# Six per-row scalars allocated in front of the transposed keys: every fp32r matmul operand starts on a multiple of 256 bytes

## The reference

```python
x_norm = (x - mu) / sqrt(var + EPS) * gamma + beta
q, k, v = x_norm @ qkv[:, :512], x_norm @ qkv[:, 512:1024], x_norm @ qkv[:, 1024:]
attn = softmax(where(causal, q @ k.T / sqrt(512), -inf))
x1 = layernorm(x + (attn @ v @ o_proj + x))
route = softmax(x1 @ wr.T); gates, idx = top_2(route), gates / sum
h2 = silu(silu(x1 @ w1.T) @ w3.T);  h = h2 @ w2.T
out = zeros; out[idx[:, k]] += gates[:, k] * h        # only rows 0 to 7 of 8192
return layernorm(x1 + out)
```

## Time and profile before

| | us |
|---|---|
| median of 3 executions | 1724.53 |
| lowest, highest | 1723.97, 1726.92 |
| span of the profiled execution | 1729.0 |
| TensorE (PE) busy in it | 1697.6 |
| VectorE, ScalarE, GpSimd busy | 788.8, 670.0, 282.0 |

### The profile page before, as it was taken

How to read it: one execution, slowest core, us unless ns; L and a number is a source line. 1 busy time by engine, 2 the same in 40 slices (tenths; PEclk the granted TensorE clock), 3 DMA queues, 4 the chain that set the end, 5 groups by cost and what they waited for, 6 DMA issues and landing times.

```text
span 1729.0 us, 23965 instructions
## 1 busy us (share of the span) xinstructions
PE 1697.6 (98%) x8179; PEld 1400.9 (81%) x8179; DVE 788.8 (46%) x2104; ACT 670.0 (39%) x1301; POOL 282.0 (16%) x491
## 2 busy tenths in 40 slices
PE   7999999999999999999999999999999999999998
PEld 5888888878888887888888888888878888888886
DVE  5454433455353454445344554534444443444443
ACT  4443333343342344334224433423344444444442
POOL 1220201121120111112011211201122121212111
PEclk9999999999999999999999999999999999999999
DMA  4111201121110112121111222112230101010100
GB/s 152 56 49 50 68 31 37 62 82 60 56 68 31 37 60 70 61 68 55 43 37 49 73 68 68 49 40 72 87 103 25 49 24 49 24 49 24 49 0 7
DMA packets 50116, 92.58 MB, mean 54 GB/s; under 512 B 5456, under 2 KB 5456, under 8 KB 50016
## 3 DMA queue, kind: packets, MB, share of 16 engines
q1 hardware_dynamic: 38064, 70.31, 11.8%
q10 hardware_dynamic: 11952, 20.99, 3.9%
HBM read 57.71 MB, written 33.57 MB: 53 GB/s over the span
## 4 chain that ended last, share of the span: by engine, by line
PE 82%; issue 12%; POOL 2%; ACT 2%; DVE 1%; DMA 1%; POOLq 0%; SPq 0%; ACTq 0%; DVEq 0%
PE psum L330 24%; PE psum L332 24%; PE psum L331 24%; PE psum L1186 3%; PE psum L1278 1%; PE psum L1124 1%; PE psum L1288 1%; PE psum L1296 1%; PE psum L1295 1%; PE psum L1287 1%; POOL expo L510 1%; POOL rstd L435 1%; ACT xin L561 1%; DMA raw<-in_wk_t 1%; ACT affine L545 0%
## 5 line engine op out<-in xcount | busy, mean ns | idle before, releaser
L330 PE MATMUL psum<-xt_hi,g_hi 128*128 128x512 f32 (+3 forms) x640 | 242.4, 379 | 0.4 <-DVE g_lo L834 0.4
L332 PE MATMUL psum<-xt_lo,g_hi 128*128 128x512 f32 (+3 forms) x640 | 232.0, 362 | 0.0
L331 PE MATMUL psum<-xt_hi,g_lo 128*128 128x512 f32 (+3 forms) x640 | 230.8, 361 | 0.0
L609 ACT ACTIVATE pt_hi<-psum 128x512 fp32r<-128x512 f32 (+3 forms) x160 | 84.8, 531 | 373.3 <-PE psum L1186 366.0
L330 PE MATMUL psum<-v_hi,pt_hi 128*128 128x512 f32 x544 | 223.0, 410 | 1.6 <-DVE pt_lo L844 1.1
L332 PE MATMUL psum<-v_lo,pt_hi 128*128 128x512 f32 x544 | 213.3, 392 | 0.0
L331 PE MATMUL psum<-v_hi,pt_lo 128*128 128x512 f32 x544 | 212.7, 391 | 0.0
L432 POOL TENSOR_TENSOR var_eps<-meanvar,eps 128x2 f32<-128x2 f32 (+1 forms) x97 | 19.3, 199 | 1070.2 <-DVE meanvar L812 1065.7
L849 DVE TENSOR_REDUCE rowmax<-psum 128x1 f32<-128x512 f32 (+3 forms) x160 | 97.7, 611 | 201.7 <-PE psum L332 200.9
L731 ACT ACTIVATE act_f<-psum 128x512 f32<-128x512 f32 x128 | 76.6, 598 | 241.4 <-PE psum L332 241.4
L510 POOL TENSOR_TENSOR expo<-euler,shifted 128x32 f32<-128x32 f32 x16 | 87.3, 5455 | 325.1 <-DVE shifted L1036 325.1
(11 more groups left out here) (146 smaller groups left out, 3379.6 us busy)
## 6 DMA issues: line engine op xcount, KB each, us to landing
xin<-in_x ACTq DMA_DIRECT2D x64, 256.0 KB, 2.8
tok<-in_x SPq DMA_DIRECT2D x64, 256.0 KB, 2.6
x_scratch<-tok SPq DMA_DIRECT2D x64, 256.0 KB, 2.1
out_dram<-tok SPq DMA_DIRECT2D x64, 256.0 KB, 2.0
x_in<-x_scratch SPq DMA_DIRECT2D x14, 1024.0 KB, 5.5
xin<-in_w_t ACTq DMA_DIRECT2D x8, 256.0 KB, 2.8
x_in<-x_scratch ACTq DMA_DIRECT2D x2, 1024.0 KB, 7.8
w_sb<-in_w_t SPq DMA_DIRECT2D x1, 1024.0 KB, 5.7
```

The costliest lines, as they stand in the source:

```text
L330: pe.matmul(o, ws, ms, start=first, stop=False, skip_group_check=True)
L331: pe.matmul(o, w_lo, ms, start=False, stop=False, skip_group_check=True)
L332: return pe.matmul(o, ws, m_lo_, start=False, stop=last, skip_group_check=True)
L609: act.activation(pt_hi[:, n % 2, 0:w], psum[:, turn_bank(turn_use(t, c)), 0:w], ACT.Copy).then_inc(pt_hi_ready, 1)
```

## The change

The six small tensors move from behind `tok` to in front of `xt_hi`. In stage 2 an unused tensor `row_scalars` of 48 floats (192 bytes, as much as the six take) holds their place, and the filler is 64 floats shorter.

```diff
+    ROW_SCALARS = 6 * 8
...
-        xt_hi = sb("xt_hi", [P, DC, S], F32R, stage01)
-        xt_lo = sb("xt_lo", [P, DC, S], F32R, stage01)
-        affine = sb("affine", [P, 512], F32, stage01)
-        tok = sb("tok", [P, SLOTS, D], F32, stage01)
         rowmax4 = sb("rowmax4", [P, 4], F32, stage01)
         rowmax = sb("rowmax", [P, 1], F32, stage01)
         bias = sb("bias", [P, 2], F32, stage01)
         sums4 = sb("sums4", [P, 2, 4], F32, stage01)
         rowsum = sb("rowsum", [P, 1], F32, stage01)
         rinv = sb("rinv", [P, 2], F32, stage01)
+        xt_hi = sb("xt_hi", [P, DC, S], F32R, stage01)
+        xt_lo = sb("xt_lo", [P, DC, S], F32R, stage01)
+        affine = sb("affine", [P, 512], F32, stage01)
+        tok = sb("tok", [P, SLOTS, D], F32, stage01)
...
+        sb("row_scalars", [P, ROW_SCALARS], F32, stage2)
         x1_in = sb("x1_in", [P, 2, GROUP, D], F32, stage2)
...
-        sb("not_yet_free", [P, 2 * DC * S - taken + (1 + SLOTS) * D + 64], F32, stage2)
+        sb("not_yet_free", [P, 2 * DC * S - taken + (1 + SLOTS) * D], F32, stage2)
```

## The result

| | before | after |
|---|---|---|
| median of the runs (us) | 1724.37 (4 runs, 1723.97 to 1726.92) | 1712.24 (4 runs, 1708.37 to 1712.39) |
| after / before | | 0.9913, 95% interval 0.99 to 0.9925 |
| span of the profiled execution | 1729.0 | 1710.4 |

A forecast was written before the change was run, and what follows sets the result against it. TensorE was taken to bound the kernel, busy 1697.6 of 1729.0 us, so time is the sum of its pitches. Gains of 8.1 + 6.0 + 0.8 + 1.1 = 16.0 us off the median 1724.5 gave 1708.5 us, range 1702 to 1718.

The forecast's parts named there:

- Term 1: `project_v` and second layer: 1536 matmuls fall from 233.3 to 226.7 ns, less 2.0 us for starts behind transposes; gain 8.1 us.
- Terms 2 and 3: `project_g`, first layer, 512-column scores: 228.9 to 226.7 ns, 6.0 us; score runs behind `attend` needn't settle anew, 0.8 us.
- Term 4: Gates and router: gate matmuls fall from 235 to 226.7 ns, 1.0 us, and the router gains 0.1; together 1.1 us.
- Term 5: Scores of 384 and 256 columns: between no gain and 0.7 us for each width; taken as zero.
- The offset to the median: Whole kernel: profiled span 4.5 us above the median of 1724.5; the same gain on the median gives 1708.5 us.
- The rival of the 16-byte lines: All streams: rests 64 and 0 both begin a 16-byte line, so no pitch changes; 1724.5 us, chance 0.07.
- The rival of `wvo`'s place: `project_v` and second layer: slow from where `wvo` lies, only the moving side counts; 7.9 us gain, about 1716.5, chance 0.14.
- The slower rival: `project_g`, first layer, 512-column scores: moving rest 0 at larger operand distance slows them to 233.3 ns; about 1736.5 us, chance 0.04.
- operands on multiples of 256: All 512-column fp32r streams: with both start bytes on multiples of 256 (rest 0) they run at 226.7 ns; chance 0.75.

The follow-up runs named there:

- run 3: Kernel before with only `wvo` (and `w3`) moved by 64 bytes, changing places with small tensors: 1717.15 us, ratio 0.9948.
- run 1: The changed kernel again, with no edit: 1708.45 us, ratio 0.9897 to the kernel before.
- run 2: Changed kernel with 64 bytes ahead of the first weight tensor, so every fp32r operand has rest 64: 1711.62 us, ratio 0.9917.
- run 8: Changed kernel with `ident`, an operand of every transpose, moved from rest 128 to rest 0: 1709.92 us, ratio 0.9906.
- run 10: Changed kernel with `mask_bf` moved behind `xin`, so some operand pairs equal round 256 differ by 256 round 512: 1709.94 us, ratio 0.9899.
- run 4: Changed kernel with `wvo` (and `w3`) alone moved by 64 bytes: 1715.84 us, ratio 0.9941.

## Why the prediction was right, point by point

The bound was read rightly: TensorE alone, by its pitches. The terms of the sum, from mean pitches over all starts of the two timelines (those over 300 ns, which hold a wait, a low clock or a start behind transposes, left out):

| term | forecast | measured |
|---|---|---|
| 1: `project_v` | | 760 x (233.35 - 227.40) = 4.5 us |
| 1: second layer | 8.1 with `project_v` | 735 x (233.20 - 227.29) = 4.3 |
| 2 and 3: `project_g` | | 768 x (229.25 - 226.69) = 2.0 |
| 2 and 3: first layer | | 752 x (229.12 - 227.73) = 1.0 |
| 2 and 3: scores of 512 | 6.8 with the two above | 1154 x (230.42 - 227.60) = 3.3 |
| 4: gates and router | 1.1 | 127 x 5.5 + 124 x 1.2 = 0.8 |
| 5: scores of 384 and 256 | 0 | 336 x (181.78 - 183.32) + 329 x (133.21 - 133.99) = -0.8 |
| `attend` | 0 | 1516 x (229.65 - 229.51) = 0.2 |
| sum | 16.0 | 15.3 |

The mechanism holds, but that the sum is only 0.7 us off is partly luck: its terms miss by -0.8 to +0.7 us, and the misses cancel.

- **Term 1** was 0.7 us too small: the 2.0 us taken off for starts behind transposes were too much. The second layer's first 11 pitches fell to 2.59 us and not to `attend`'s 2.63, and the means of 227.4 and 227.3 ns, 0.6 to 0.7 above the final pitch, make the loss about 1.0 us.
- **Terms 2 and 3** came in 0.5 us short, most of it in the first layer (1.0 us, where 768 x 2.2 ns = 1.7 were counted): "the settling behind transposes is alike on both sides here, so nothing comes off" doesn't hold there; 227.73 ns is 1 ns above its final pitch.
- **Term 4** came out near its forecast by luck. It priced the gates' fall from 235 ns by the move of their own tensors to rest 0, but both their rests were 64 before, and so equal already. What slowed them was the second layer around them, as run 3 shows, and that was cured by the same change.
- **Term 5** has the wrong sign. Both ends of its bound were gains or nothing; the narrow scores lost 0.8 us, and did so in each profile with equal rests (384 columns: 183.2 to 183.3 ns in the changed kernel and runs 1, 2, 8 and 10, 181.8 in the kernel before and run 3). Why they do is open. The nearest rows, streams of 512 columns, were no guide to a shorter matmul.
- **The offset to the median.** The forecast of 1708.5 took its gain off a median of three executions and carried the 4.5 us between profiled span and median along. That difference is larger than 4.5 us, since in every execution of the kernel before with both on record the time is 1.8 to 1.9 us above the span: the profiled one took some 1729.0 + 1.8 = 1730.8 us. It is mostly granted clock, 0.995 over its span: at the 1.4 us for each 0.001 that run 1 gives, an execution at 0.995 would take an estimated 1729.9 us. Three of the changed kernel's first four executions were granted 0.997, so their median of 1712.2 lies 3.7 us above the forecast; run 1's, at 0.999 to 1.000, is 1708.45, on it. The sum of the pitches isn't touched by this.
- **The rival of the 16-byte lines** fell. By that rule of the Trainium skill (SBUF — State Buffer, section "Specifications (TRN2)") nothing would have moved; the eight differences of the table are all multiples of 32, so that every operand begins such a line, and their pitches range from 226.7 to 234.0 ns. The trace disagrees with what was drawn from the rule: the lines of 16 bytes alone don't set these pitches.
- **The rival of `wvo`'s place** fell with the result, `project_v` at 226.6 ns with `wvo` unmoved, and again by runs 3 and 4. The sentence of the Trainium skill that leaned its way (TensorE: Matmul & The Clock Gate, section "Step-by-step: what each phase is for"), that loading the next weights takes no read bandwidth from the running matmul, doesn't carry what was drawn from it, that a stationary rest costs nothing: in runs 3 and 4 the moving tensor is in the same place and only the stationary one's differs, 226.9 and 229.4 ns. Why the pitch depends on it, by the reads of the weight load or something else, no run here shows.
- **The slower rival** was right that a new place can make the streams slower, and wrong about where: not at equal rests, but at rests 96, 128, 192 and 224, which the same six tensors would have given with fewer of them moved.
- What was reasoned too narrowly is the rule itself: "operands on multiples of 256" isn't needed (run 2). The rows with both rests at 64 said so already, at 227.5 ns; the text listed them beside the gate pair's 235 ns, which seemed to say the contrary, and drew nothing from it.

## What to carry to other kernels

In a kernel that TensorE bounds, read pitches from start to start in the timeline and sort them by where the operands stand; the mean durations of the groups hide them. For fp32r matmuls of 512 columns with new weights each time, give the stationary and the moving tensor the same rest round 256 bytes, also in the long streams around short ones. Small tensors between large ones decide it, and here a stray 32 bytes cost as much as most larger differences. Neither needs to start on a multiple of 256. Before a profiled span is set against a median, compare their granted clocks.

## What the runs showed of the hardware that was not expected

- In long streams of 512-column fp32r matmuls the pitch depends on the difference of the two operands' addresses (stationary less moving) round 256 bytes, with a sign: 226.7 ns at 0, 229 at 192, 232 to 234 at the six other multiples of 32. A short stream's pitch goes also with the rests of the long stream beside it: 227.4 to 228.0 ns for the gates where those are equal, 231.5 to 232.9 where they aren't.
- Narrow matmuls don't follow that rule: 384 columns go from 181.8 ns on average (difference 192) to 183.3 when the rests become equal, and to 184.4 at rest 96 (difference 160).
- Where TensorE's loop over the batches jumps back, it stands still for 2.1 to 2.4 us, and the clock may be at the lower level right behind it. The two jumps of the kernel before in the stretches above (start us, us, instruction, idle before):

```profile
375.86 0.54 PE L1186 MATMUL psum<-ident,probs 128*128 128x128 f32 x3 [2.20 <-issue]
...
683.63 0.54 PE L1186 MATMUL psum<-ident,probs 128*128 128x128 f32 x3 [2.41 <-issue]
```

and those of the changed kernel:

```profile
371.50 0.71 PE L1189 MATMUL psum<-ident,probs 128*128 128x128 f32 x3 [2.13 <-issue]
...
677.00 0.55 PE L1189 MATMUL psum<-ident,probs 128*128 128x128 f32 x3 [2.37 <-issue]
```

The lower level followed both jumps in the kernel before, the first alone in the changed one, and neither in run 1, whose first jump has the same length (2.17 us). What decides it isn't shown here.
